# Half of the second GEMM's sum as seven half-size products, its partial output kept in DRAM

## The reference

```python
r, k, v = x, fside, fside                       # (4, 1024, 1024)
tf    = sigmoid(sum(time_emb))                  # one number for each batch element
decay = exp(-exp(w)) * (0.5 + 0.5 * tf)
...                                             # a forward and a backward scan over the 1024 tokens
base  = sigmoid(r) * num / max(den, 1e-8)
mix   = base * (0.8 + 0.2 * tf)                 # (4, 1024, 1024)
h = einsum('bsd,fd->bsf', mix, W1)              # first GEMM,  D = 1024 -> F = 4096
a = gelu(clip(round(h / 0.1)) * 0.1)
out = x + einsum('bsf,df->bsd', a, W2)          # second GEMM, F = 4096 -> D = 1024
```

## Time and profile before

| | |
|---|---|
| median of 3 runs | 1775.26 us (1774.64 to 1775.8) |
| profiled execution, its own time | 1775.51 us |
| its span, first to last instruction | 1773.2 us |
| TensorE busy | 1695.2 us, 96% |
| VectorE busy | 1118.6 us, 63% |
| ScalarE busy | 897.5 us, 51% |
| moved by DMA | 321.16 MB, mean 181 GB/s |

### The profile page before, as it was taken

The page is one execution under the profiler, slowest core; times in us unless marked ns, Lnnn a source line. Parts: engine busy times, 40 slices in busy tenths (PEclk is TensorE's granted clock), DMA queues, the critical chain, the costliest instruction groups (busy, mean ns, idle before and its releaser), DMA issues.

```text
span 1773.2 us, 27144 instructions
## 1 busy us (share of the span) xinstructions
PE 1695.2 (96%) x10946; PEld 1073.6 (61%) x10946; DVE 1118.6 (63%) x1547; ACT 897.5 (51%) x1384; POOL 24.6 (1%) x44
## 2 busy tenths in 40 slices
PE   1579999999999999999999999999999999999998
PEld 0134444885468844787448854588546874488645
DVE  8977865777565765677766675677756666632211
ACT  3467532786238741587327761388424773245300
POOL 0000020000000000000000000000000000000000
PEclk9789999999999999999999999999999999999999
DMA  9858885664566544665546644556456654455442
GB/s 243 205 155 234 297 289 178 213 210 144 160 191 189 189 149 139 213 197 184 162 156 204 196 146 158 190 179 208 159 168 186 188 173 157 147 168 166 136 133 83
DMA packets 109380, 321.16 MB, mean 181 GB/s; under 512 B 12736, under 2 KB 12992, under 8 KB 108736
## 3 DMA queue, kind: packets, MB, share of 16 engines
q1 hardware_dynamic: 106560, 296.28, 52.1%
q0 software_dynamic: 2688, 23.07, 5.8%
HBM read 310.91 MB, written 48.23 MB: 203 GB/s over the span
## 4 chain that ended last, share of the span: by engine, by line
PE 87%; DVE 0%; issue 0%; ACT 0%; DVEq 0%
PE ps L588 48%; PE ps L532 39%; PE ps L599 1%; DVE ND L1067 0%; ACT mo L747 0%; DVE mo L1132 0%; DVE RCP L1024 0%; DVE m_st L1031 0%; DVE y_out L1184 0%; DVE a L1117 0%; DVE ND L1021 0%; DVE a L1121 0%; DVE a L1119 0%; DVE y_out L1195 0%; DVE chk_full L1203 0%
## 5 line engine op out<-in xcount | busy, mean ns | idle before, releaser
L588 PE MATMUL ps<-act,w_ring 128*128 128x512 f16 x4032 | 874.0, 379 | 0.7 <-DVE y_out L1184 0.7
L532 PE MATMUL ps<-mo,w_ring 128*128 128x256 f16 x6272 | 688.1, 273 | 0.0
L588 PEld LDWEIGHTS ps<-act,w_ring 128*128 128x128 f16 x4032 | 394.5, 98 | 472.1 <-issue 1.1
L532 PEld LDWEIGHTS ps<-mo,w_ring 128*128 128x128 f16 x6272 | 613.5, 98 | 75.7
L1175 DVE SCALAR_TENSOR_TENSOR act<-a,act 128x1024 f16<-128x1024 f32 x128 | 156.4, 1222 | 133.2 <-ACT act L806 133.2
L1184 DVE SCALAR_TENSOR_TENSOR y_out<-ps,x_in 128x512 f32<-128x512 f32 x63 | 43.5, 691 | 227.4 <-PE ps L588 158.9
L814 ACT ACTIVATE q<-chk_full 128x1024 int8<-128x1024 f32 x64 | 67.2, 1050 | 151.7 <-DMA chk_full<-in_w_dram 151.6
L800 ACT ACTIVATE a<-q 128x1024 f32<-128x1024 int16 x128 | 135.3, 1057 | 15.3 <-DVE act L1175 10.9
L806 ACT ACTIVATE act<-a 128x1024 f16<-128x1024 f32 x128 | 134.2, 1049 | 0.9
L692 ACT ACTIVATE EE<-V 128x512 f32<-128x512 f32 x64 | 40.0, 625 | 158.3 <-DMA V<-in_fside_dram 157.7
L509 PE MATMUL ps<-mo,w_ring 128*128 128x512 f16 x128 | 43.1, 513 | 71.2 <-DVE mo L1110 71.2
(11 more groups left out here) (102 smaller groups left out, 1194.2 us busy)
## 6 DMA issues: line engine op xcount, KB each, us to landing
w_ring<-w1s SPq DMA_DIRECT2D x168, 512.0 KB, 3.7
w_ring<-w_half SPq DMA_DIRECT2D x144, 512.0 KB, 4.3
chk_full<-in_w_dram SPq DMA_DIRECT2D x64, 512.0 KB, 4.6
V<-in_fside_dram SPq DMA_DIRECT2D x64, 256.0 KB, 4.8
R<-in_x_dram SPq DMA_DIRECT2D x64, 256.0 KB, 5.0
w_half<-in_w_dram POOLq DMA_DIRECT2D x16, 1024.0 KB, 8.1
x_in<-in_x_dram SPq DMA_DIRECT2D x64, 256.0 KB, 5.6
out_dram<-y_out SPq DMA_DIRECT2D x63, 256.0 KB, 4.8
```

What stands on the lines that cost most here:

```text
L532: mm = pe.matmul(dst[:, f, :], wp_ring[:, k, r, f, q, :], mo[:, op, q, p, :], start=(fresh and f == 0 and q == 0 and p == 0), stop=(q == K ...
L588: mm = pe.matmul(y_ps[y][:, :], w2_ring[:, k, f, :], act[:, a, p, :], start=(a == 0 and p == 0), stop=(a == FT - 1 and p == 1))
```

## The change

In blocks 1 to 7 the sum over units 0 to 3 (`SPLIT = 4`) in the second GEMM is now also made as seven half-size products, in two passes `e` over half of the output channels each; the sum over units 4 to 7 stays plain. The partial output, x included, is written to `y_part` in DRAM in quarters (`y_quad`, `store_quad`), and is read back where x was read before (`residual`). The operands of these products are seven combinations of activation quarters (`quad_sums`, `quads_hi_*`, `quads_lo_*`), which take the place of `act_hi` and `act_lo` for units 0 to 3; the weight sums are made in block 0 (`weight_sums2`) and stored to `w2s`. `y_product` is one product, 32 matmuls of 256 columns. All engines' lists are written anew (`chained_block`), the tiles of the next mix are placed earlier in the block, and the banks of outputs 0 to 7 are now banks 0 to 7. Which hidden features form a unit changes too (`w1_pair`), and buffers are shared in another way (`tt`, `tq`, `xy`).

```diff
+    SPLIT = 4
+    KH2 = 2 * SPLIT
+    CHAIN = STEPS + 2
...
+            def y_product(n, e, dst, k, op, fresh, units, stored):
+
+                for i in range(2):
+                    for s in units:
+                        if e == 0 and i == 0:
+                            pe.wait_ge(s_glo, 4 * quad_unit(n, s) + stored)
+                        for j in range(2):
+                            for p in range(2):
+                                mm = pe.matmul(dst[:, i, :], wy_ring[:, k, i, 2 * s + j, :], ao[:, s, op, j, p, :],
...
+            for n in range(1, BLOCKS):
+                products_15(n, 0)
+                products_26(n, 0)
+                for s in range(1, SPLIT + 1):
+                    products_15(n, s)
+                    products_73(n, s - 1)
+                    products_26(n, s)
+                    product_4(n, s - 1)
+                begun = y_15_begin(n)
+                products_73(n, SPLIT)
+                y_15_end(n, begun)
+                y_26(n, 0)
+                product_4(n, SPLIT)
+                y_15(n, 1)
+                y_73(n, 0)
+                y_26(n, 1)
+                y_4(n, 0)
+                products_15(n, SPLIT + 1)
+                y_73(n, 1)
+                products_26(n, SPLIT + 1)
+                y_4(n, 1)
+                for s in range(SPLIT + 2, STEPS):
+                    products_15(n, s)
+                    products_73(n, s - 1)
+                    products_26(n, s)
+                    product_4(n, s - 1)
...
```

ScalarE's list for units 0 to 4:

```diff
+            def chained_block(n, nxt, g0, at):
+                seed(hid(n, 0))
+                spill_p5(hid(n, 0))
+                if nxt:
+                    tile_group_between(g0)
+                quantise11(n, 0)
+                for s in range(1, SPLIT + 1):
+                    if s >= 2:
+                        quantise21(n, s - 2)
+                        gelu(n, s - 2, 1)
+                    seed(hid(n, s))
+                    if s >= 2:
+                        quads_hi_2(n, s - 2)
+                    spill_p5(hid(n, s))
+                    if s >= 2:
+                        quads_hi_t(n, s - 2)
+                    if nxt and s in (2, 4):
+                        tile_group_between(g0 + s // 2)
+                    quantise12(n, s - 1)
+                    gelu(n, s - 1, 0)
+                    quantise11(n, s)
+                    quads_hi_11(n, s - 1)
```

VectorE's new operations and its list (`mix(t, ...)` is `part(..., g0 + t)`):

```diff
+            def quad_sums(n, s):
...
+                v.tensor_tensor(tq[:, 0:2, :], a_quads[:, :, 1, :], a_quads[:, 0, :, :], ALU.subtract).then_inc(s_gt, 1)
...
+                v.tensor_tensor(tq[:, 2, :], a_quads[:, 1, 1, :], tq[:, 0, :], ALU.subtract).then_inc(s_gt, 1)
...
+                v.tensor_tensor(tq[:, 3, :], a_quads[:, 1, 0, :], tq[:, 2, :], ALU.subtract).then_inc(s_gt, 1)
...
+                mix(0, 0, 1)
+                seed_u4(hid(n, 0))
+                mix(0, 2, 3)
+                quantise22(n, 0)
+                seed_u4(hid(n, 1))
+                for s in range(2, SPLIT + 1):
+                    quad_sums(n, s - 2)
+                    quads_lo_11(n, s - 2)
+                    quads_lo_2(n, s - 2)
+                    mix(s // 2, 0 if s % 2 == 0 else 2)
+                    quantise22(n, s - 1)
+                    quads_lo_t(n, s - 2, 0)
+                    quads_lo_t(n, s - 2, 1)
+                    mix(s // 2, 1 if s % 2 == 0 else 3)
+                    seed_u4(hid(n, s))
...
+                y21(n, 1)
+                mix(5, 1)
+                quantise22(n, SPLIT + 1)
+                act_lo(n, SPLIT + 1, 0)
+                mix(5, 2)
+                seed_u4(hid(n, SPLIT + 2))
...
+                residual_sum(n, 1)
+                mix(7, 0)
                 if nxt:
+                    convert(n + 1, 1)
                 residual_sum(n, 2)
-                check(at + 2)
+                mix(7, 1)
+                check(at + 4)
                 residual_sum(n, 3)
+                mix(7, 2, 3)
+                check(at + 5)
                 residual_sum(n, 4)
                 if nxt:
+                    divide(g0 + 7)
+                    convert(n + 1, 2)
                 residual_sum(n, 5)
                 check(at + 6)
                 if nxt:
+                    convert(n + 1, 3)
+                residual_sum(n, 6)
                 check(at + 7)
                 if nxt:
                     residual_sum(n, 7)
```

More of the change, by code:

```diff
@@ L390, in ffn_block @@
             def ffn_block(n):
                 nxt = n + 1 < BLOCKS
[L392 to L402, removed]
-                    if s == 1 and n > 0:
+                g0, at = CT * (n + 1), DT * n
@@ L435, in _ @@
+                residual(n, 5)
+                load_check(at + 6)
+                ring_load()
+                store(n, 4)
+                residual(n, 6)
+                ring_load()
+                store(n, 5)
+                residual(n, 7)
+                load_check(at + 7)
+                ring_load(2)
+            ffn_first()
+            for n in range(1, BLOCKS):
                 ffn_block(n)
@@ L856, in hidden_block @@
+                    gelu(n, s - 1, 0)
                     quantise11(n, s)
-                    if s >= 1:
-                        act_hi(n, s - 1, 0)
-                quantise21(n, LAST - 1)
-                gelu(n, LAST - 1, 1)
-                act_hi(n, LAST - 1, 1)
+                    quads_hi_11(n, s - 1)
+                quantise21(n, SPLIT - 1)
+                gelu(n, SPLIT - 1, 1)
+                quads_hi_2(n, SPLIT - 1)
+                quads_hi_t(n, SPLIT - 1)
+                seed(part_y(n, 0))
@@ L862, in hidden_block @@
+                quantise12(n, SPLIT)
+                gelu(n, SPLIT, 0)
+                act_hi(n, SPLIT, 0)
+                spill_p5(part_y(n, 0))
+                if nxt:
+                    tile_group_between(g0 + 3)
+                quantise21(n, SPLIT)
+                gelu(n, SPLIT, 1)
+                act_hi(n, SPLIT, 1)
+                seed(part_y(n, 1))
+                check_i8(at)
+                spill_p5(part_y(n, 1))
                 if nxt:
                     tile_group_between(g0 + 4)
+                check_i8(at + 1)
@@ new lines, in chained_block @@
+                seed(hid(n, SPLIT + 1))
+                spill_p5(hid(n, SPLIT + 1))
+                check_i8(at + 2)
+                if nxt:
+                    tile_group(g0 + 5)
+                quantise11(n, SPLIT + 1)
+                seed(hid(n, SPLIT + 2))
+                spill_p5(hid(n, SPLIT + 2))
+                quantise12(n, SPLIT + 1)
+                gelu(n, SPLIT + 1, 0)
+                quantise11(n, SPLIT + 2)
+                act_hi(n, SPLIT + 1, 0)
+                quantise21(n, SPLIT + 1)
@@ new lines, in chained_block @@
+                gelu(n, SPLIT + 1, 1)
+                seed(hid(n, LAST))
+                act_hi(n, SPLIT + 1, 1)
+                spill_p5(hid(n, LAST))
+                quantise12(n, SPLIT + 2)
+                gelu(n, SPLIT + 2, 0)
+                quantise11(n, LAST)
+                act_hi(n, SPLIT + 2, 0)
+                quantise21(n, SPLIT + 2)
+                gelu(n, SPLIT + 2, 1)
+                act_hi(n, SPLIT + 2, 1)
+                if nxt:
+                    tile_group_between(g0 + 6)
@@ L1266, in _, with convert @@
[L1266 to L1286 removed]
+            def convert(n, q):
+                operand_sums(n, q)
+                operands_lo(n, q)
```

970 lines of the change are left out of this document (666 added, 304 removed).

## The result

The changed kernel takes 1802.73 us (median of 4 runs, 1801.47 to 1809.92) against 1775.52 us before: the ratio is 1.0162, with a 95% interval of 1.0136 to 1.0189. It is 27 us slower where 10 were forecast: the direction was right, the size was not. The profiled execution has a span of 1799.2 us, 26.0 more than before.

A forecast was written before the change was run, and what follows sets the result against it. TensorE, busy in 96% of the span, was taken to bound the kernel. From 1775.5 us, 44.4 saved and 53.9 of new waits gave 1785 us, range 1754 to 1806 leaving out a tenth on each side.

The forecast's parts named there:

- TensorE's saving: Second GEMM of blocks 1 to 7: half-size products save 6.35 us a block, 44.4 us in all.
- The new waits: TensorE waits for VectorE and ScalarE in blocks 0 to 6: 53.9 us in sum.
- the stores costed at nothing: Block 0: the eight stores of weight sums cost nothing, since the ring runs ahead.
- the chain through `check(6)` and the seed: Block 0's end: later sums delay `check(6)` by 2.5 us; through load, `check_i8` and seed TensorE waits 2.1 in block 1.
- The waits for x in even blocks: End of even blocks: VectorE waits for x of output 4, 6.0 us from issue; a wait of 0.8 us.
- the sum: Whole kernel: 1775.5 us less 44.4 saved plus 53.9 of new waits gives 1785 us.
- rival (d): TensorE's clock falls at the 17 gaps over 1.5 us, up to 2.6 each, 44 us: 1829 us; chance 0.05.
- this case: Whole kernel: the sum as counted holds, 1785 us, own range 1774 to 1797; chance 0.50.
- (a): All blocks: waits are not carried on, only head waits stay, sum 18 us: 1749 us; chance 0.25.
- (b): Saving and waits nearly cancel, with cheap `quad_sums` and waits a sixth smaller: 1765 to 1778 us; chance 0.10.
- (c): Passes: DMA becomes the wait if only 255 GB/s is had, 35 us over seven blocks: 1820 us; chance 0.10.

The follow-up runs named there:

- The last run: Changed kernel, VectorE and ScalarE lists reordered, block 0 starting as in the change, third tile's exponentials behind unit 3's operands: 1752.19 us, ratio 0.9877.
- The two runs on the kernel before: Kernel before, only order changed in blocks 1 to 6: `forward` ahead of `seed_u4(0)`, 1785.77 us; `backward` ahead of it too, 1805.00 us.
- the run of 1768.04: Kernel with block 0 as changed, plus `quads_lo_t` ahead of the mix part that waits for ScalarE in units 2 to 4: 1768.04 us, ratio 0.9960.
- the kernel with block 0 as changed: Changed kernel with lists reordered in units 0 to 4, unit 6 and the checks, but `weight_sums2(0)` still ahead of `convert(1, 0)`: 1779.14 us, ratio 1.0025.

## Why the prediction was half right

**TensorE's saving: right.** Block 7, which makes no mix, has no wait from 1590.67 to 1792.8: 202.1 us, as forecast (202.0). The last run's sum closes with the 44.4 us to within 0.8.

**The new waits: right in their sum, and within the units also in place and cause; at the starts of blocks they were not.** Us forecast and measured beside each other:

| place | forecast | measured |
|---|---|---|
| odd blocks, units 0 to 4 and `y_15` | 27.3 | 28.4 |
| even blocks, the same | 8.4 | 7.7 |
| `products_73(6)`, six blocks | 8.1 | 8.4 |
| start of the block behind an odd one | 3.0 | 5.9 |
| start of the block behind an even one | 2.4 | 0 |
| block 0, and the start of block 1 | 4.6 | 5.6 |
| sum | 53.9 | 56.0 |

The sum is better than its terms. In odd blocks' units 0 to 4 errors partly cancel: block 1's `seed_u4(0)` waited 5.44 us instead of 2.5, because ScalarE's spill there waited 3.19 us for the stores of `w2s` (the stores costed at nothing), and the waits behind it were each 0.1 to 0.3 us shorter than forecast. At the starts of blocks 2, 4 and 6 the last `convert` for the new block was late (0.28 to 0.96 us) as well as ScalarE's seed (0.84 to 2.15). At the start of block 1 the chain through `check(6)` and the seed, forecast at 2.1 us, did not hold TensorE; 1.20 us came from `residual_sum(0, 6)`, which itself had waited 1.19 for its x, and 1.98 from `convert`. The waits for x in even blocks did not come.

```profile
311.28 0.69 DVE L1686 SCALAR_TENSOR_TENSOR xy<-ps,xy 128x512 f32<-128x512 f32 x1 [1.19 <-DMA xy<-in_x_dram]
...
322.27 0.60 ACT L1101 ACTIVATE sp<-ps 128x512 f32<-128x512 f32 x1 [3.19 <-DMA w2s<-sp]
```

**The step that failed is the sum:** "53.9 us of new waits against 44.4 saved". It priced a gap at its length. The trace has 13.7 us more: 5.8 for the drain of the matmul ahead of each of 35 gaps, which no step of mine had, and 7.9 for the slow clock, which I had put into rival (d) as all or nothing: 2.6 us behind each of 17 gaps, or none. The two runs on the kernel before priced it: about 1.6 us, behind one gap in three at 2.3 to 2.8 us and behind each at 5.6. With these prices, and the five falls that only the trace after tells, the sum is 1785 + 5.8 + 5 x 1.6 = 1799, and with the waits' 2.1 us 1801. My own range for this case, 1774 to 1797, spanned the waits' counting error alone; it had to take in what a gap costs beyond its length.

**The rivals.** (a), waits not carried on, was wrong for the kernel as changed. Its 1749 us is near the last run's 1752 by chance, since other waits are left there than (a) named. (b) fell: `quad_sums` takes 1.22 us, the value taken, and the waits were not smaller than counted. (c) fell: in block 1's passes (386 to 463) TensorE had no wait while DMA moved 266 GB/s, slices of up to 323 GB/s passed, and no DMA released TensorE. (Two of its numbers were off: the mean of the busiest three slices in a row is 273 GB/s, not 255, and 18 pieces of 512 KB are 9.4 MB, not 8.9.) At second hand two transfers of block 1's start mattered, the store and the x shown above. (d) was right in kind, at a sixth of its price. The rule of the Trainium skill (TensorE: Matmul & The Clock Gate, "Why this matters for your kernels") that idle gaps between bursts bring back the slow clock agrees with these traces from single gaps of some 2 us on, though not for each of them. The page allows somewhat longer gaps before that happens; the traces show it behind shorter ones, and they decide.

**Why it was slower at all** is thereby shown: 56 us of waits from the order of VectorE's and ScalarE's lists, with a quarter on top for the gaps' own cost, outweigh 44 us of saving. That the orders carried it is shown by the runs (50 us came back with the same instructions, of which 9 were the first GEMM's head and units 0 to 4, 15 the other orders, 11 and 16 the operands of units 2 and 3). Open is why the clock fell behind some gaps of 2.0 to 3.1 us and not behind others of the same length.

## What to carry to other kernels

When work goes off the busiest engine onto covered ones, walk the covered engines' queues through the shortest unit, not through the block's average; and where one edge is mended, look at the next edge of the same queue before counting the gain, since here 22 us of waits only moved on, until VectorE's order (9 us) and then the exponentials ahead of unit 3 (7 us) were changed too. Price a gap in TensorE's stream above its length: here some 0.17 us each and, behind 2 us or two shorter gaps close together, now and then 1.6 more. Keep instructions that wait for another engine behind those whose inputs are ready, and check which loads stand in order behind the step that is moved (10 us here).

## What the runs showed of the hardware

The clock's fall has nearly the same price for gaps of 2.3 and 5.6 us: bursts of 752 matmuls of 256 columns took 82.25 us at the full clock and 83.74 to 83.92 behind such gaps (85.02 in block 1). At the same length (2.27 us) the clock fell in one block and held in two. Two gaps that are both shorter can bring it too, with only 8 matmuls between them. Blocks 2 and 4 of the kernel with block 0 as changed have the same two gaps, 1.5 and 1.2 us; the granted clock was 1.00 from 594 to 607 and 0.87 from 1011 to 1024:

```profile
597.08 8.03 PE L813 MATMUL ps<-act,w_ring 128*128 128x256 f16 x72 [1.22 <-DVE act L1676]
...
1014.19 9.63 PE L813 MATMUL ps<-act,w_ring 128*128 128x256 f16 x72 [1.22 <-DVE act L1676]
```

The kernels with many gaps spread more from run to run than the kernel before (1.5 us over 15 runs), but not by the gaps' number: the changed one with 36 gaps from 225 us on ranged over 8.5 us in 4 runs and the run of 1768.04 with 16 over 8.1 in 6, with the mean clock (0.978 to 0.983, and 0.979 to 0.985), while the one of 1779.14 with 24 ranged over 2.9 in 10.
